# The third mixture's 32 gate multiplies issued on GpSimd instead of VectorE, with new issue lists

## What is computed

```python
h = h + _L0_attn_ref(_layernorm(h), ...)      # retention
h = h + _L0_ffn_ref(_layernorm(h), ...)       # mixture 0: 16 experts, top 2, relu
h = h + _L1_attn_ref(_layernorm(h), ...)      # attention in blocks of 8
h = h + _L1_ffn_ref(_layernorm(h), ...)       # mixture 1: 32 experts, top 1, relu
h = h + _L2_attn_ref(_layernorm(h), ...)      # linear attention and a small MLP
h = h + _L2_ffn_ref(_layernorm(h), ...)       # mixture 2: 8 experts, top 2, gelu
h = h + _L3_attn_ref(_layernorm(h), ...)      # linear recurrence
h = h + _L3_ffn_ref(_layernorm(h), ...)       # votes: sign of gated weight sums

# mixture 2
out = tokens
for e in range(8):
    hid = gelu(tokens @ w1[e] + b1[e])
    out = out + combine[:, e:e + 1] * (hid @ w2[e] + b2[e])
```

## Time and profile before

| | us |
|---|---|
| median of 3 runs | 692.06 (692.03 to 700.5) |
| the profiled execution | 693.0 |
| its span, first to last instruction | 691.2 |
| 128x512 multiplies of `gated2` on DVE | 32 |
| granted TensorE clock, mean | 0.912 |

### The profile page before, as it was taken

The page is one execution under the profiler, slowest core; times in us unless marked ns, Lnnn a source line. Parts: engine busy times, 40 slices in busy tenths (PEclk is TensorE's granted clock), DMA queues, the critical chain, the costliest instruction groups (busy, mean ns, idle before and its releaser), DMA issues.

```text
span 691.2 us, 8576 instructions
## 1 busy us (share of the span) xinstructions
PE 584.9 (85%) x3086; PEld 328.2 (47%) x3086; DVE 487.5 (71%) x921; ACT 304.9 (44%) x529; POOL 183.6 (27%) x146
## 2 busy tenths in 40 slices
PE   6783529999999999988888875777899999999995
PEld 5562316444345355455744543444545554445431
DVE  0548689997778987988688899898988853323320
ACT  0311231110011123353446654314576689999872
POOL 6784000000220411442326243734132410000000
PEclk9996669999999999999699988756999999999995
DMA  8310314689854542100000122102130000000001
GB/s 206 115 23 1 93 40 134 207 202 294 240 192 138 174 131 77 46 2 1 1 1 0 41 84 79 46 0 76 51 123 1 1 1 0 1 0 16 16 1 30
DMA packets 30778, 49.86 MB, mean 72 GB/s; under 512 B 8400, under 2 KB 8656, under 8 KB 30736
## 3 DMA queue, kind: packets, MB, share of 16 engines
q1 hardware_dynamic: 29136, 46.82, 22.5%
q10 hardware_dynamic: 576, 1.45, 0.9%
q0 software_dynamic: 1024, 1.05, 0.7%
HBM read 47.86 MB, written 1.44 MB: 71 GB/s over the span
## 4 chain that ended last, share of the span: by engine, by line
PE 48%; DVE 29%; issue 8%; POOL 7%; ACT 5%; DMA 2%; DVEq 0%; ACTq 0%
PE ps L1040 9%; PE ps L779 7%; PE ps L1018 7%; PE ps L772 5%; PE ps L773 3%; DVE hid L1301 3%; POOL sq L445 3%; POOL inv_std L478 3%; PE ps L894 3%; DVE total L1196 2%; DVE xn L1199 2%; DVE xs L1233 2%; PE ps L767 2%; PE ps L1029 2%; DVE var L1205 2%
## 5 line engine op out<-in xcount | busy, mean ns | idle before, releaser
L715 ACT ACTIVATE hid<-ps 128x512 bf16<-128x512 f32 x256 | 135.5, 624 | 32.9 <-PE ps L1040 30.9
L478 POOL TENSOR_TENSOR inv_std<-var,neg_half 128x8 f32<-128x8 f32 x44 | 75.8, 1724 | 185.1 <-DVE var L1205 184.8
L1040 PE MATMUL ps<-xs,w3z 128*128 128x512 f32 x256 | 117.5, 523 | 5.9 <-ACT hid L715 4.6
L772 PE MATMUL ps<-xs,up_hi 128*128 128x512 f32 x192 | 95.6, 498 | 22.5 <-DVE hid L1301 14.2
L1018 PE MATMUL ps<-hid,kbin 128*128 128x512 bf16 x256 | 100.0, 393 | 0.2 <-ACT hid L715 0.2
L1503 DVE TENSOR_TENSOR xs<-ps,big_a 128x512 fp32r<-128x512 f32 x64 | 43.4, 688 | 74.5 <-PE ps L1029 74.4
L772 PEld LDWEIGHTS ps<-xs,up_hi 128*128 128x128 f32 x192 | 37.4, 195 | 89.1 <-issue 36.3
L773 PE MATMUL ps<-xs,up_lo 128*128 128x512 f32 x192 | 78.2, 407 | 0.0
L624 ACT ACTIVATE hid<-ps,kd 128x512 f32<-128x512 f32 x64 | 43.9, 687 | 71.1 <-PE ps L913 40.9
L779 PE MATMUL ps<-hid,kb 128*64 128x512 f32 x256 | 67.5, 622 | 0.0
L1040 PEld LDWEIGHTS ps<-xs,w3z 128*128 128x128 f32 x256 | 49.1, 193 | 35.1 <-ACT hid L715 20.0
(11 more groups left out here) (254 smaller groups left out, 990.2 us busy)
## 6 DMA issues: line engine op xcount, KB each, us to landing
big_a<-gates_out SPq DMA_DIRECT2D x64, 256.0 KB, 3.8
fm<-gates_out SPq DMA_DIRECT2D x32, 256.0 KB, 3.9
xT<-gates_out SPq DMA_DIRECT2D x32, 256.0 KB, 3.8
big_a<-gates_out SPq DMA_DIRECT2D x32, 128.0 KB, 2.9
fm<-gates_out SPq DMA_DIRECT2D x16, 128.0 KB, 2.9
xT<-gates_out SPq DMA_DIRECT2D x16, 128.0 KB, 3.0
hid<-wup SPq DMA_DIRECT2D x4, 391.0 KB, 13.0
out<-h SPq DMA_DIRECT2D x4, 256.0 KB, 2.6
```

Source lines behind the costliest of these rows:

```text
L478: G.tensor_tensor(inv_std[u][:, :], var[u][:, :], neg_half[:, :], ALU.pow).then_inc(norm_rstd[u], 1)
L715: act.activation(sg[u][:, n % SUMS, :], b0, ACT.Sign).then_inc(s_made[u], 1)
L772: pe.matmul(b0, up_hi[:, a:a + P], xs[u][:, l, :], start=True, stop=False)
L1040: pe.matmul(b0, w3z[:, j, 2 * b:2 * (b + 1), :].rearrange("p i o -> p (i o)"), xs[u][:, l, :], start=True, stop=True).then_inc(w_made[u], 1)
```

## The change

`gated2` leaves the VectorE program and becomes part of the GpSimd program, after the residual of mixture 2 (`PL_RES2`) and ahead of the power for `LN_A3`. Operands, semaphores and the four gate places stay the same. All five strings are new; the number of steps of SP, ACT and PE is unchanged, POOL's grows from 126 to 158 and DVE's falls from 826 to 794.

```diff
 TURNS = {
...
     "POOL": (
-        "sttttttttt0ttt1tttttttttttttt0ttt23123000000111101121222230233332301000030010111211112322222333030202330"
-        "0331110111222222333333"
+        "sttttttttt0ttt1tttttttttt2tt0ttttt1323000000101111212223212333303230010000002111131100202122103032032300"
+        "231230101031310110212220212113332213313232312233323233"
     ),
...
@@ -494,6 +494,14 @@
+                    def gated2(i):
+                        m, l = divmod(i, LANES)
+                        yield
+                        pool.wait_ge(hid_made[u], HM_M2 + i)
+                        pool.wait_ge(gate_in[u][i % SLOTS], gate_landed(HG_M2, i))
+                        to = hid[u][:, l, m % RING, :]
+                        G.tensor_tensor(to, slots[u][i % SLOTS], to, ALU.mult).then_inc(hid_gated[u], 1)
+
...
@@ -526,6 +534,8 @@
                     G.tensor_tensor(y[u][:, :, :], h[u][:, :, :], xn[u][:, :, :], ALU.add).then_inc(pool_step[u], 1)
+                    for i in range(LANES * MT):
+                        yield from gated2(i)
                     yield from rstd(LN_A3)
...
@@ -1301,14 +1311,6 @@
-                    def gated2(i):
-                        m, l = divmod(i, LANES)
-                        yield
-                        dve.wait_ge(hid_made[u], HM_M2 + i)
-                        dve.wait_ge(gate_in[u][i % SLOTS], gate_landed(HG_M2, i))
-                        to = hid[u][:, l, m % RING, :]
-                        V.tensor_tensor(to, slots[u][i % SLOTS], to, ALU.mult).then_inc(hid_gated[u], 1)
-
...
@@ -1453,8 +1455,6 @@
                     yield from top2(G_M2, E2, AC_EXPG2)
-                    for i in range(LANES * MT):
-                        yield from gated2(i)
```

More of the change, by code:

```diff
@@ L46 @@
     "SP": (
-        "st000001111100001001010100100101010100101010210222201010210210210203121212123333121212123331231222332323"
-        "3232323232323232323323333333330000000001111111112222222223333333330123"
+        "st000001111100000010101001010001010010210222201020120120120130120120212333311212212333312121212333131212"
+        "2323323232323232323233333333330000000001111111112222222232333333330123"
     ),
     "POOL": (
-        "sttttttttt0ttt1tttttttttttttt0ttt23123000000111101121222230233332301000030010111211112322222333030202330"
@@ L52 @@
-        "0331110111222222333333"
+        "sttttttttt0ttt1tttttttttt2tt0ttttt1323000000101111212223212333303230010000002111131100202122103032032300"
+        "231230101031310110212220212113332213313232312233323233"
     ),
     "ACT": (
-        "sss01000111203001010111222ttt333222323323300000001010011101010010201120002012023110310202131132131220133"
-        "10101231022233222021223001321332132032133301103020302302313010120110320331001112231312313202112200220302"
-        "02032013023031012303022013013101030013110102030110120123301011010010212210230102012332102101023023123012"
@@ L58 @@
-        "30101230231231023101023021321302130120320321321301201320321320312103201320321031210230132032103121023013"
-        "203210310213213232131213213232131213213213232323232323232323232323232333333333"
+        "sss01000111200010311011222ttt323322323323300000000100111120020101020210230113020233013120130310221131112"
+        "13302212020312121302323203332300133222131033301002010202113023013011210312200031213312121232102323123003"
+        "21120003032032030130220300110300003131010100211010102201101031020212132013012020213210310310230212310210"
@@ L60 @@
+        "31023021321021031032031231021023013023123102102301302312301201203103231231021023103203123102102301302301"
+        "231212313231231212313231231212313231231212313123232233232322332323223233333333"
     ),
     "PE": (
-        "sbbbbbbbbbbbbbbbbbbbbbbbbbbbbbbbtbbbbbbb0bbb01bb0101bbbbbbbb1bbb0bb000101111t22012tt03003030020130010110"
-        "02011002012200101100101100301100103213020101300101100201121002201322102130021210210012201102112212112233"
-        "33102031203212103212131323032312321332232332232033223203321302131230132203233201302302302302130301133030"
@@ L65 @@
[L65 to L69, removed]
@@ L70 @@
-        "11032211003322001133221003322110023311022311002233001133221003322110023311022311002233001133221003322110"
-        "23311032211332211332213322113321132211332211332213322113321132211332213322133223323223322332233223323223"
-        "3223322332233232233223322332332333333333333333333"
+        "sbbbbbbbbbbbbbbbbbbbbbbbbbbtbbbbbbbbb0bbb0b1bb01b01bbbbbbbbb1bbbb0b000101111t2021tt202003030030200103120"
+        "01202100110100000103101030123302010100101200120212101030123001210211220201220110012011220201223333331121"
@@ new lines @@
+        "22112102230330311031231121223031231231233122132033223203323202332232332231213320312330313303003303133032"
+        "00232031200101023133130101210312012101111213213322202022310123122321332132333330300323212121323030030003"
+        "20221110030300131101022201101013121323101202122312322302301220100013030003201020331003300300200030023001"
+        "00210000000100231001101123001100113001001101100110032110031002101112001100211002210022113220112200112300"
+        "11220032210032211033221100233110033110022133002231102233110022110023311002213300221103322113002211002331"
@@ L73 @@
+        "10033122003311022331100322110022330021133001223301122331100322110022330021133001223301122330011322001122"
+        "00332110033122033112233110032211002233112003312200331102233110032211002233002113301223301122331122311223"
+        "31123312233112233112231122331123312233112233112231122331123312233112233112231122331233122332233223223323"
+        "3223322332232233233223322332232332333333333333333"
     ),
     "DVE": (
-        "s000sss011101100222020011033301310012000000000000001300000101111111111111111111111tttttttttttttttttttttt"
@@ L76 @@
[L76 to L80, removed]
@@ L81 @@
-        "23202132032022301213122021032230130333333333310122101201302133121331312332310112113232230231123122320322"
-        "22231220223233123023133223033331323303333213033231023102310231023120312031203123012312312323233233"
+        "s000sss011101100222020011023013100100000000000000130000010311311111111111111111111tttttttttttttttttttttt"
+        "tt202tt0tttt202202tt0t2t30103210213033202210222231022202220102312022232301201330333333330103333201203312"
+        "03313230101201202120101201202102030303031002102102102330310312001201023023001030102031203201312312103231"
@@ new lines @@
+        "02312131213021302003020013302321232131123212312311213211311212333123221323133231211320110102201323022333"
+        "23333020203330223220023202030203301311031333331300011010100011021221012100120000130303000020302002320001"
+        "00012123212322131211321333313311321111111231121111121111112222332330200220323032223202220322222203222022"
+        "20033003330333033333333000333333011101100110111111110222211121022123233203121231222033223123302333233130"
+        "322323130233130213021032103210321032103210321032132132132132323233"
```

## The result

| | before | after |
|---|---|---|
| median of the first measurement, us | 693.07 | 716.44 |
| ratio, 95% interval | | 1.031 (1.023 to 1.039) |
| the same, measured again | | 1.024 (1.014 to 1.034) |
| profiled execution, span, us | 691.2 | 715.6 |

A forecast was written before the change was run, and what follows sets the result against it. VectorE was taken to set the pace from 380 to 480 us, with PE full afterwards. Relief of 20.7 us less 6.4 and 5.4 gave about 9 us off 693.0: 684 us, range 671 to 702.

The forecast's parts named there:

- The stretch that bounds: From 380 to 480 us VectorE, busy 88.4 of 100 us, sets the pace; 29.8 us of PE's idle time lie there.
- the durations: Each moved 128x512 multiply on GpSimd takes 1.45 us, ends 1.27 and 1.8; 32 make 46 us.
- the stands: VectorE steps lengthened while a wide GpSimd operation runs; between nothing and 1.07 us per operation, 0.28 taken.
- at 0.28 each 6.4 us: VectorE time lost to the 23 moved multiplies between 380 and 500 us; range 0 to 24.6 us.
- the sum: 20.7 us relief less 6.4 lost on VectorE gives 14.3; less 5.4 for longer multiplies, 9 us off the end.
- The value of relief: VectorE's 14.3 us relief in 380 to 500 us, below PE's 23.4 us of waits, counted fully toward the end.
- The occupation of GpSimd: GpSimd's busy time from 380 to 560 us grows from 67.9 to about 114 of 180 us and fits.
- 5.4 us for seven pieces of the chain: Chain of waits in 380 to 500 us passes seven multiplies, each 0.77 us longer on GpSimd.
- rival (c): GpSimd's in-order list becomes the limit from 430 to 530 us: 15.5 us later, 708.5 us; chance 0.15.
- (b): Lengthened VectorE steps, up to 1.07 us per moved multiply, eat the relief: 690 to 702 us; chance 0.22.
- Idle time that PE loses before 480 comes off the end: PE is full from 480 us on, so idle time removed earlier shortens the run almost one for one.
- Cost at nothing: New strings in the first 380 us cost nothing, 3 us either side, since PE is full there.

The follow-up runs named there:

- The run with the port free: Changed kernel, each moved GpSimd multiply replaced by two 128x640 memsets (nothing read in SBUF) and a 16-column multiply: 697.51 us, 1.012 of the kernel before.
- the relief on the old strings: Kernel before with all its strings, its VectorE multiply cut to 16 of 512 columns, nothing given to GpSimd: 689.82 us, 0.990.

## Why the prediction was wrong

**The stretch that bounds and the durations were right.** VectorE's load from 380 us on matters: 17 us off it gave 7 us (1 to 13), and 22.7 us of stands put on it (32 extra multiplies against as many pairs of memsets) cost 3.1%, 21 us. The multiply took 1.28 us in the median and up to 2.2 against the 1.45 taken; GpSimd came to 227 us against "about 230".

**The step that failed first: the stands were mis-sized, 0.28 us each, measured 0.62.** This is the term "at 0.28 each 6.4 us". It was a mean over the 44 wide operations of the whole run, and it left out the stands of L1310 itself on the ground that L1310 would be gone. But the turn that L1310 held on VectorE isn't gone: other steps with two SBUF inputs follow in its place and can stand as well. With L1310's 5.1 us counted, before has 17.3 / 44 = 0.39. In the stretch where the new multiplies were to lie, 400 to 500 us, 13 of its 18 wide operations of GpSimd made a step of VectorE stand, 11.8 us in all: 0.65 for each, close to the 0.62 measured. At 0.65 the 23 multiplies would have cost 15.0 us, and the sum would have come to 20.7 - 15.0 - 5.4, nothing gained. That alone does not give a loss of 17 to 21 us; the two steps below were wrong too. 19.9 us for 32, where the same rate of 0.28 gives 9, eat most of the 27 that left; the rest comes from the other operations of GpSimd, whose stands rose from 17.3 - 5.1 = 12.2 to 18.1 us, presumably because VectorE's next steps arrive at other moments. VectorE was forecast at 470 us busy and came to 491.5; some 5 us of that are lengthenings too small or of a kind that this count leaves out.

**The value of relief was mis-sized too.** "Less than the 23.4 us for which PE waited, so PE's waits don't cap it" took VectorE's time as time off the end. Measured with nothing in exchange, it is 7 us for 17, about 0.4 (0.1 to 0.8 by the interval). The strings keep all other steps in their old order, and the next engine in line can take over the wait; that this is why so little arrives is argued, not shown. With a factor of 0.4 the net gain of the sum would have been nothing even with the stands at 0.28.

**The occupation of GpSimd was taken for free as long as it is not full.** The sum charged 5.4 us for seven pieces of the chain. The run with the port free shows some 16 us by ratio (4 to 27) and 7 to 8 by spans and medians, second product included; the memsets on the old strings, with the product's path untouched, show 8 (4 to 11). The rival (c) was to decide at "some 90% busy". Between 430 and 540 us after the change:

```profile
430.00:540.00 110.00, 85.93 (x313) 46.44 (x316) 94.21 (x143) 48.91 (x76) 78.98 (x55) 0.75 0.20 61
```

GpSimd is busy 79.0 of 110 us, 72%, and the queue costs already. The powers of the norms stand in the same in-order list, so a power behind a multiply can come later by its length, then the norm on VectorE, then PE; no run took this way apart by itself.

**Neither rival alone, but (b) and (c) together.** Both parts are clear of zero: 10 to 12 us of port and 7 to 16 of occupation, against some 7 of relief. That nets 10 to 21 us, where the change is slower by 17 to 21 (ratio 1.024 to 1.031). The signs are shown; how the loss divides is not, as the port's share on the old strings, 21 us, shows too. Rival (b) at its full stand price ended at 702, since it had the port without the occupation; (c) came to 708.5 without the port. I gave them separate chances and never the sum.

**"Idle time that PE loses before 480 comes off the end" left out the clock.** Of the 24.4 us of span, 3.0 are idle time of PE and 21.4 are busy time for the same work. In the trace the granted clock is at 1.2 GHz for 113 us of PE's busy time after, for 73 us before; at 2.4 GHz half of either is saved, and the 20 us between 56.7 and 36.4 are that difference. Less that half, PE's busy time would be 548.5 us before and 549.6 after, so the clock accounts for the whole rise in its busy time. Much of the time at 1.2 GHz comes where PE waited (380 to 480 us, some 32 and 33 us of busy time), and after the change also in 480 to 560: 23.5 us, where there was none before. Not all of the rise is there: 120 to 320 us has 18.6 us against 3.4 and the first 120 have 22.8 against 14.6, and the kernel with the short multiply has these two as well (18.0 and 26.1), so they come with the new strings. In all that kernel has 81.4 us of busy time at 1.2 GHz against 113.3 with the full multiply. Its row shows the stretch from 380 on with PE's gaps fewer:

```profile
380.00:560.00 180.00, 148.06 (x663) 85.11 (x670) 148.86 (x271) 100.37 (x165) 88.28 (x83) 0.90 0.15 48
```

663 matmul records at a clock of 0.90 in these 180 us; the changed kernel has 285 + 285 = 570, at 0.78 and 0.85 (25 records of the whole run are missing in either trace). That the gaps lower the clock is read from these rows; no run changed the clock alone, so how the loss divides between gap and clock as cause stays argued.

**"Cost at nothing" for the new strings held in a way that I hadn't meant.** PE did lose 5.7 us in 120 to 320 us (188.1 against 193.8), but the run with the multiply cut short, at 0.990, is as fast as the relief on the old strings, so the new ones make up for it when the multiply is short. What isn't settled is how much of the difference between the whole (1.024 to 1.031) and the move on the old strings (1.007) is the strings' fault: they put more multiplies next to the powers and the steps with two SBUF inputs (22 stands against 17, which is counted; why is argued), and I did not try the same steps in a third order.

## What to carry to other kernels

Before moving elementwise work from VectorE to GpSimd, count what VectorE does beside it: with VectorE 81 to 91% busy from 380 to 480 us, 15 to 24 of 32 multiplies of two SBUF operands made a VectorE step with two SBUF inputs stand, and in the changed kernel the 0.68 us saved for each was given back as 0.62. Price a stand by the part of the run where the new operation will lie, and count those of the operation that is moved, since its place in the queue is taken by another. Measure first, with the operation cut short in place, what its removal is worth at all: here 1% (0.2 to 1.9), and every version with the full multiply on GpSimd ended slower than the kernel before.

## What the runs showed of the hardware

- The blocking goes in both directions. A 128x512 VectorE step with both inputs in SBUF that meets a 128x512 tensor_tensor of GpSimd ends 0.55 us after it, in up to 1.81 instead of 0.68 us; the short gating steps end 0.02 to 0.09 us after it in nearly every case. A GpSimd operation of this size that starts during such a VectorE step takes 1.7 to 1.8 us in most cases instead of 1.27, and over 2 in a few (2.20 after the change).
- Two memsets of 128x640 on GpSimd (1.26 us) made no VectorE step with two SBUF inputs stand in 32 places, in either of two kernels; a multiply of about the same length did in 15 to 24 of 32.
- A multiply of only 128x16 on GpSimd takes 0.22 us in the median, 0.35 in the mean and 0.76 at the longest (the kernel with the short multiply).
- PE's busy time for the same matmuls moved by 21.4 us between two kernels, its idle time by 3.0; 20 of the 21 are the difference in time at 1.2 GHz (113.3 against 72.8 us).
